# Scores from three stationary operands of at most three heads, with q gathered in two rounds and projected one iteration ahead

## The chip, the cores and the metric

The kernel runs on one core of one Trainium2 chip. The metric is the device time of one execution in microseconds. Engines are named as in the profile: PE is TensorE's matmul side and PEld its weight loads, DVE is VectorE, ACT is ScalarE, POOL is GpSimd, SP is the engine that issues DMAs.

## What is computed

Cross attention of 4 batches of 2048 query rows over 77 context rows, 16 heads of 32, everything in float32, followed by an output projection, a residual and a layer norm:

```python
qs = (q @ wq).reshape(Bq, Lq, H, HD).transpose(0, 2, 1, 3)
ks_ = (k @ wk).reshape(Bq, Lk, H, HD).transpose(0, 2, 1, 3)
vs = (v @ wv).reshape(Bq, Lk, H, HD).transpose(0, 2, 1, 3)
scores = jnp.einsum('bhqd,bhkd->bhqk', qs, ks_) / jnp.sqrt(jnp.float32(HD))
scores = jnp.where(mask[:, None, :, :], -jnp.inf, scores)
attn_w = jax.nn.softmax(scores, axis=-1)
attn = jnp.einsum('bhqk,bhkd->bhqd', attn_w, vs)
attn = attn.transpose(0, 2, 1, 3).reshape(Bq, Lq, H * HD)
out = attn @ wo + q
mu = jnp.mean(out, axis=-1, keepdims=True)
var = jnp.mean((out - mu) ** 2, axis=-1, keepdims=True)
return (out - mu) / jnp.sqrt(var + EPS) * gamma + beta
```

Here x has shape (4, 2048, 512), the context (4, 77, 512), and the four weights (512, 512).

## The kernel before

The 8192 query rows are 64 tiles of 128 rows (`T` = 64). Four tiles make a block of 512 rows; there are 16 blocks, and 16 tiles (`TB`) to a batch. All five engines run a program written out by hand, one iteration per tile t, and meet through semaphores only. Each engine executes its own list strictly in order.

Every float32 product is made of three products of shorter numbers: a matrix is split into a high part (x becomes `xh`, q becomes `qh`/`qn`, k becomes `khc`) and the low rest (`xl`, `ql`, `klc`), and high·high, high·low and low·high are added up in one PSUM bank.

In iteration t, PE does this:

- `scores(t, (0, 1))` and `scores(t, (2, 3))`: the scores of tile t, one group g of four heads at a time, into one of two banks.
- `project_q(i)`: 12 matmuls of 512 columns that make quarter m = i mod 4 of q for block i // 4. Four such calls make the q of one block. It waits for all four low slices of that block's x: `pe.wait_ge(g_xl, 4 * (i // 4 + 1))`.
- `project_o(t - 6)`: 12 matmuls of 512 columns, the output projection of an older tile.
- `weigh_v`: in iterations with t mod 4 = 1 (from 5), the attention-weighted values of four older tiles.
- `transpose_p(t - 1, half)`: five transposes each, of the normalised weights.

An iteration has two places for a projection: the first after `scores(t, (0, 1))`, the second after `scores(t, (2, 3))`. For t mod 4 = 0, 1, 2 the first holds `project_o(t - 6)` and the second `project_q(t + 4)`; for t mod 4 = 3 it is `project_q(t + 4)` first and `project_o(t - 6)` second.

ACT rounds x to `xh` (`keep_x(t + 8)`), copies q out of PSUM (`keep_q`), copies transposes and values, and computes the exponentials. DVE masks the scores and takes their maximum (`mask_max`, L789 and L795), sums rows and takes reciprocals (`row_sums`, L802 and L804), makes the low parts of q and of the values (`low_q` L777, `low_a` L811) and adds the residual. POOL runs, in iteration t, `deviation(t - 7)` (L990 to L996), `normalise(t - 1, 1)` (L977, L979), `gain_and_shift(t - 8)` (L1001, L1003), `low_x(t + 8)` (L962, the low slice of x) and `normalise(t, 0)`.

From block 2 on, one group of scores takes three matmuls: low q against high k, all four heads, 308 columns (L463), and twice 154 columns for two heads each (L469), where the stationary operand `qd` holds the high q of two heads twice over, and the moving operand `kd` holds their high k above their low k. `double_q(i)` builds `qd` with four DMAs per quarter of q; `place_kh` and `place_kd` build the k operands of a batch with DMAs. All of them are issued by SP, whose list also has the loads of x (`load_slice(t + 9)`, L260), the residual rows, the masks and the stores.

Of the kernel before, what the change touches and what calls it, by code (L numbers as in the profile page):

```python
# [11 lines left out]
GW = 4 * LK  # L12
PW = 2 * LK
NG = 4
HH = H // 2
# [23 lines left out]
LAG = 6  # L39

KD_AT = {4: 0, 12: 1, TB + 4: 2, 2 * TB + 4: 3}

KH_AT = {8: 1, TB + 8: 2, 2 * TB + 8: 3}
# [20 lines left out]
def cross_attention_layernorm(nc, x, xT, ctxT, mask, wq, wk, wv, wo, gamma, beta, out):  # L64
# [12 lines left out]
    with ctx:  # L77
# [13 lines left out]
        kh = sb("kh", [P, NG + 2, GW], f32r)  # L91
        kd = sb("kd", [P, 2, NG, 2, PW], f32r)
# [23 lines left out]

        ql0 = sb("ql0", [P, NG, D], f32r)
        ql1 = sb("ql1", [P, NG, D], f32r)


        with ExitStack() as start:
# [6 lines left out]
            early("place_qd", [P, 2 * NG * D - KT * D - KT * NB * LK])  # L128
# [7 lines left out]
            early("place_qn", [P, KT, D])  # L136
# [5 lines left out]
        qd = sb("qd", [P, 2, 2, NG, D], f32r)  # L142
        qn = sb("qn", [P, NG, D], f32r)
# [5 lines left out]
        ql = (ql0, ql1)  # L149
# [3 lines left out]
        qk = [ah, qd[:, 1, 0]] + [qn] * (NBLK - 2)  # L153

        kl = kd[:, 1].rearrange("p g u k -> p g (u k)")

        def kh_at(b, g):

            return g if g < 2 else g + 2 * (b % 2)
# [33 lines left out]
        d_kh = [sem(f"d_kh{i}") for i in range(2)]  # L193
        d_kl, d_kd = sem("d_kl"), [sem(f"d_kd{i}") for i in range(2)]
        d_qd = [sem(f"d_qd{g}") for g in range(NG)]
# [56 lines left out]
        def _(sp):  # L252
# [35 lines left out]
            def spread(dst, src, sig):  # L288

                for j in range(4):  # L290
                    rows = slice(32 * j, 32 * j + 32)
                    sp.dma_start(dst[rows, :, j * LK:(j + 1) * LK].bitcast(f32), src[rows].bitcast(f32)).then_inc(sig, 16)

            def place_kh(b, i):

                if i == 0:
                    sp.wait_ge(p_s, NG * (TB * b - 1) + 2)
                elif b >= 2:
                    sp.wait_ge(p_s, NG * TB * (b - 1))
                at = kh_at(b, 2 * i)  # L300
                spread(kh[:, at:at + 2], khc[:, 2 * i:2 * i + 2, b], d_kh[i])

            def place_kd(b):

                if b >= 1:
                    sp.wait_ge(p_s, NG * max(8, TB * (b - 1)))
                for v, src in enumerate((khc, klc)):
                    for j in range(4):
                        rows = slice(64 * v + 32 * (j % 2), 64 * v + 32 * (j % 2) + 32)
                        sp.dma_start(kd[rows, b % 2, :, j // 2, j % 2 * LK:(j % 2 + 1) * LK].bitcast(f32),  # L310
                                     src[32 * j:32 * j + 32, :, b].bitcast(f32)).then_inc(d_kd[b % 2], 16)

            def double_q(i):

                blk, m = i // 4, i % 4
                if blk >= 3:
                    sp.wait_ge(p_s, NG * 4 * (blk - 1))
# [17 lines left out]
            spread(kh[:, 0:NG], khc[:, :, 0], d_kh[0])  # L335
# [739 lines left out]
```

## Time and profile before

| | us |
|---|---|
| median of 3 runs | 617.94 (617.9 to 618.48) |
| profiled execution: span from the first to the last instruction | 616.2 |
| median less this span | 1.7 |
| PE busy in it | 599.4 (97%) |
| DVE, ACT, POOL busy | 520.4, 506.6, 491.3 |

The span covers the instructions; the time of an execution has some more around it. A row of a timeline gives the start in microseconds from the span's start, the duration, the engine, the line, the operation with out<-in, and how many equal instructions the row merges; in brackets stands the idle time before it and what ended that. PE's durations are latencies and overlap: the distance from one start to the next is what a matmul costs.

### The profile page before, as it was taken

How to read it: one execution, taken by the hardware profiler on the slowest of the kernel's cores; microseconds unless marked ns; L12 is line 12 of the kernel's file. 1: busy time of each engine (PE TensorE's matmuls, PEld its weight loads, DVE VectorE, ACT ScalarE, POOL GpSimd, SP SyncE). 2: the span in 40 equal slices, each digit the busy share in tenths (PEclk: the TensorE clock that was granted, in tenths of full speed). 3: DMA queues.
4: the chain of work that ended last, by engine and by line, in shares of the span. 5: the costliest groups of instructions: out<-in, count | busy, mean ns of one | idle time of the engine just before them, and what ended most of it. 6: DMA issues, size and time to landing. Idle time of an engine off the chain costs nothing.

```text
span 616.2 us, 12956 instructions
## 1 busy us (share of the span) xinstructions
PE 599.4 (97%) x3856; PEld 476.5 (77%) x3856; DVE 520.4 (84%) x1060; ACT 506.6 (82%) x1558; POOL 491.3 (80%) x639
## 2 busy tenths in 40 slices
PE   9998999999999999999999999999999999998995
PEld 7876687877878787787878788787878878786763
DVE  6677798898888889888888988898888889888888
ACT  6788888988888898888889888888988888886851
POOL 4587458897979889797979979797997979687784
PEclk9999999999999999999999999999999999999999
DMA  8621475463655546355654645555463555643103
GB/s 281 198 67 52 131 192 178 124 187 111 170 146 160 171 141 180 106 171 143 164 165 120 180 129 168 149 160 159 123 176 116 163 151 138 206 106 102 53 36 119
DMA packets 62165, 89.22 MB, mean 145 GB/s; under 512 B 20368, under 2 KB 20880, under 8 KB 62096
## 3 DMA queue, kind: packets, MB, share of 16 engines
q1 hardware_dynamic: 62096, 88.39, 50.1%
q8 instruction: 32, 0.52, 0.4%
q14 instruction: 37, 0.30, 0.1%
HBM read 39.53 MB, written 16.78 MB: 91 GB/s over the span
## 4 chain that ended last, share of the span: by engine, by line
PE 82%; DVE 6%; POOL 4%; ACT 4%; issue 2%; POOLq 0%; DVEq 0%; ACTq 0%
PE bank L433 27%; PE bank L529 24%; PE bank L479 7%; PE bank L469 6%; PE bank L463 5%; PE bank L502 4%; PE bank L483 2%; PE bank L507 2%; ACT pr L639 2%; PE bank L409 1%; DVE al L811 1%; PE bank L460 1%; ACT ah L607 1%; POOL pn L977 1%; DVE pr L789 1%
## 5 line engine op out<-in xcount | busy, mean ns | idle before, releaser
L639 ACT ACTIVATE pr<-pr,nm 128x77 f32<-128x77 f32 x1024 | 270.0, 349 | 39.5 <-DVE nm L795 35.9
L977 POOL TENSOR_TENSOR pn<-pr,rec 128x512 f32<-128x512 f32 x128 | 134.8, 1053 | 77.7 <-DVE rec L804 76.1
L789 DVE SCALAR_TENSOR_TENSOR pr<-msk,bank 128x308 f32<-128x308 uint8 x256 | 109.3, 468 | 33.6 <-PE bank L469 28.6
L802 DVE TENSOR_REDUCE sm<-pr 128x8 f32<-128x616 f32 x128 | 100.6, 786 | 9.7 <-ACT pr L639 9.3
L795 DVE TENSOR_REDUCE nm<-pr 128x8 f32<-128x616 f32 x128 | 101.7, 795 | 4.4
L529 PE MATMUL bank<-woh,ah 128*128 128x512 f32 x256 | 103.8, 405 | 1.4 <-DVE al L811 1.3
L433 PE MATMUL bank<-xh,wqh 128*128 128x512 f32 x256 | 103.2, 403 | 0.0
L607 ACT ACTIVATE ptr<-bank 128x512 f32<-128x512 f32 (+1 forms) x256 | 95.7, 428 | 8.8 <-PE bank L479 8.7
L529 PE MATMUL bank<-woh,al 128*128 128x512 f32 x256 | 101.3, 396 | 0.0
L529 PE MATMUL bank<-wol,ah 128*128 128x512 f32 x256 | 101.1, 395 | 0.0
L433 PE MATMUL bank<-xh,wql 128*128 128x512 f32 x256 | 100.3, 392 | 0.0
L433 PE MATMUL bank<-xl,wqh 128*128 128x512 f32 x256 | 100.0, 391 | 0.0
L463 PE MATMUL bank<-kh,ql 128*128 128x308 f32 x224 | 82.4, 368 | 2.2 <-DVE pr L789 2.2
L962 POOL TENSOR_TENSOR xl<-xraw,xh 128x512 fp32r<-128x512 f32 x58 | 75.5, 1303 | 10.1 <-ACT xh L607 10.0
L479 PE MATMUL bank<-ident,pn 128*128 128x128 f32 x512 | 77.0, 273 | 4.9 <-ACT ptr L607 3.5
L479 PEld LDWEIGHTS bank<-ident,pn 128*128 128x128 f32 x512 | 61.9, 140 | 21.6 <-issue 5.4
L469 PE MATMUL bank<-kd,qd 128*128 128x154 f32 x448 | 77.4, 254 | 0.0
L1003 POOL TENSOR_TENSOR y<-y,bet 128x512 f32<-128x512 f32 x56 | 72.2, 1290 | 4.4
L469 PEld LDWEIGHTS bank<-kd,qd 128*128 128x128 f32 x448 | 74.6, 190 | 0.0
L1001 POOL TENSOR_TENSOR y<-y,gam 128x512 f32<-128x512 f32 x56 | 72.1, 1288 | 0.0
L662 ACT ACTIVATE y<-z,rs 128x512 f32<-128x512 f32 x56 | 45.8, 817 | 30.7 <-POOL rs L996 29.6
L811 DVE TENSOR_TENSOR al<-bank,ah 128x512 fp32r<-128x512 f32 (+1 forms) x68 | 40.6, 642 | 26.8 <-ACT ah L607 26.8
(94 smaller groups left out, 1020.5 us busy)
## 6 DMA issues: line engine op xcount, KB each, us to landing
qd<-qn SPq DMA_DIRECT2D x224, 128.0 KB, 2.6
xraw<-xT SPq DMA_DIRECT2D x58, 256.0 KB, 3.4
xres<-x SPq DMA_DIRECT2D x58, 256.0 KB, 2.8
out<-y SPq DMA_DIRECT2D x56, 256.0 KB, 2.0
ptr<-xT SPq DMA_DIRECT2D x6, 256.0 KB, 9.0
zt<-x SPq DMA_DIRECT2D x6, 256.0 KB, 4.1
out<-zt SPq DMA_DIRECT2D x6, 256.0 KB, 2.0
wk_sb<-wk SPq DMA_DIRECT2D x4, 256.0 KB, 4.8
```

What stands on the lines that cost most here:

```text
L433: last = nc.tensor.matmul(misc_bank(("q", i))[:], w[:, k, m * P:(m + 1) * P], s[:, blk % 2, k, :], start=(k == 0 and n == 0), stop=(k == K ...
L463: nc.tensor.matmul(o[:, 0:GW], ql[blk % 2][:, g, cols], kh[:, kh_at(t // TB, g), :], start=True, stop=False)
L469: last = nc.tensor.matmul(o[:, u * PW:(u + 1) * PW], qd[:, blk % 2, u, g, cols], kd[:, t // TB % 2, g, u, :], start=False, stop=(u == 1))
L479: last = nc.tensor.transpose(PTB[0][:, s * P:(s + 1) * P], pn[:, half, s, :], ident[:])
L529: last = nc.tensor.matmul(o[:], w[:, k, r * P:(r + 1) * P], s[:, k, :], start=(n == 0), stop=(w is al and i == KT - 1))
L607: return nc.scalar.activation(dst, src, ACT.Copy)
L639: last = nc.scalar.activation(s, s, ACT.Exp, bias=nm[:, t % 2, h:h + 1], scale=1.0)
L789: nc.vector.scalar_tensor_tensor(out=pr[:, 4 * g:4 * g + 4, :], in0=msk[:, m % MR, t % 4, :].unsqueeze(1).broadcast_to([P, 4, LK]), scalar ...
L795: nc.vector.tensor_reduce(nm[:, t % 2, HH * half:HH * half + HH], pr[:, HH * half:HH * half + HH, :], AX.X, ALU.max, negate=True).then_inc ...
L802: nc.vector.tensor_reduce(sm[:, t % 2, hs], pr[:, hs, :], AX.X, ALU.add).then_inc(v_sum, 1)
L962: nc.gpsimd.tensor_tensor(xl[:, n // KT % 2, n % KT, :], x_of(n), xh[:, n // KT % 2, n % KT, :].bitcast(f32), ALU.subtract).then_inc(g_xl, 1)
L977: nc.gpsimd.tensor_tensor(pn[:, half, 0:4, :].rearrange("p s (e k) -> p (s e) k", e=2), pr[:, hs, 0:KM], rec[:, t % 2, hs].unsqueeze(2).br ...
```

## The change

- **Scores.** From block 2 on, the three stationary operands lie in `qs[:, buffer, part]`, 128 rows made of four 32-row pieces each. Part 0 holds high q of heads 0, 1, 2 and again of head 1; part 1 holds low q of heads 0, 1, 2 and high q of head 0; part 2 holds high q of head 3, its low q, its high q again, and high q of head 2. The moving operand `ks` has nine segments of 78 columns (`KW`, one more than 77). The three matmuls of a group then have 156, 234 and 234 columns.
- **Copies of q.** ACT and DVE write `qh` and `ql` straight into parts 0 and 1. `gather_q(i)` makes four copies of 32 rows into part 2; `fill_q(i)` waits for these to land and makes two more copies over the rows that were read. That is six DMAs of 64 KB per quarter in place of four of 128 KB.
- **Copies of k.** `place_k` makes twelve DMAs per batch, for batch 0 all twelve at the end of SP's iteration 4, for the others in two parts of six.
- **q projection.** From t = 3 on, the second place of an iteration holds `project_q(t + 5)` and the first `project_o(t - 6)`, also for t mod 4 = 3. Iteration 3 gets one projection more, and `project_o(54)` moves from after `scores(60, (0, 1))` into the second place of iteration 59. `keep_q(t + 4)` and `low_q(t + 4)` follow in iteration t. `low_x`, `keep_x` and `load_slice` stay where they are.
- The first two blocks keep their three matmuls over four heads, with 312 columns where there were 308.

```diff
+SA, SC, SH = 0, 3, 5
+K_PARTS = [(0, SC + 1, 3, 0), (1, SC + 1, 3, 0), (2, SC + 1, 3, 1), (3, SC, 2, 1),
+           (0, SA, 0, 0), (1, SA + 1, 1, 0), (2, SA + 2, 2, 0), (3, SA, 0, 0),
+           (0, SH, 0, 1), (1, SH + 1, 1, 0), (2, SH + 2, 2, 0), (3, SH + 1, 1, 1)]
+KN = len(K_PARTS)
+KS_AT = {4: (0, 0, KN), 10: (1, 0, KN // 2), 12: (1, KN // 2, KN)}
...
         for t in range(T - 4):
-            if t % 4 == 3:
+            if t <= 3:
                 misc += [("q", t + 4)]
             misc += [("o", t - LAG)] if t >= LAG else []
             misc += [("v", VALUES[t])] if t in VALUES else []
-            if t % 4 < 3:
-                misc += [("q", t + 4)]
+            if 3 <= t < T - 5:
+                misc += [("q", t + 5)]
...
+            def gather_q(i):
+
                 sp.wait_ge(a_qh, i + 1)
+                copy_q(i, 2, 0, 0, 3, d_qc)
+                copy_q(i, 2, 2, 0, 3, d_qc)
+                copy_q(i, 2, 3, 0, 2, d_qc)
+                sp.wait_ge(v_ql, i + 1)
+                copy_q(i, 2, 1, 1, 3, d_qc)
+
+            def fill_q(i):
+
+                sp.wait_ge(d_qc[i % 4], 64 * (i // 4 - 1))
+                copy_q(i, 1, 3, 0, 0, d_qa)
+                copy_q(i, 0, 3, 0, 1, d_qa)
...
-                if t in KD_AT:
-                    place_kd(KD_AT[t])
...
-                if 5 <= t <= T - 4 and t % 4 > 0:
-                    double_q(t + 3)
...
+                if 4 <= t < T - 4:
+                    gather_q(t + 4)
...
+                if 4 <= t < T - 4:
+                    fill_q(t + 4)
...
+                if t in KS_AT:
+                    place_k(*KS_AT[t])
...
-                    nc.tensor.matmul(o[:, 0:GW], ql[blk % 2][:, g, cols], kh[:, kh_at(t // TB, g), :], start=True, stop=False)
...
-                    for u in range(2):
-                        last = nc.tensor.matmul(o[:, u * PW:(u + 1) * PW], qd[:, blk % 2, u, g, cols],
-                                                kd[:, t // TB % 2, g, u, :], start=False, stop=(u == 1))
...
+                    for n, (part, head, seg, heads) in enumerate(((2, 2, SC, 2), (1, 0, SA, 3), (0, 0, SH, 3))):
...
+                        last = nc.tensor.matmul(o[:, KW * head:KW * (head + heads)], qs[:, blk % 2, part, g, cols],
+                                                ks[:, t // TB % 2, g, seg:seg + heads, :].rearrange("p h k -> p (h k)"),
+                                                start=(n == 0), stop=(n == 2), skip_group_check=True)
...
-                if t % 4 == 3:
+                if t == 3:
                     project_q(t + 4)
                 elif t >= LAG:
                     project_o(t - LAG)
...
-                if t % 4 == 3:
-                    if t >= LAG:
-                        project_o(t - LAG)
+                if t < 3:
+                    project_q(t + 4)
+                elif t == T - 5:
+                    project_o(T - 10)
                 elif t >= LAG or t not in VALUES:
-                    project_q(t + 4)
+                    project_q(t + 5)
...
-            project_o(T - 10)
```

PE in iteration 11 (t mod 4 = 3) before: the end of `project_q(15)` in the first place, the transposes (L479, L483), the scores (L463, L469), and the start of `project_o(5)` (L529) in the second place:

```order
L433 MATMUL bank<-xl,wqh 128x512
L433 MATMUL bank<-xh,wql 128x512
L479 MATMUL bank<-ident,pn 128x128 [waits a_pt,g_norm]
L479 MATMUL bank<-ident,pn 128x128 x3
L483 MATMUL bank<-ident,pn 128x128
L463 MATMUL bank<-kh,ql 128x308 [waits v_st,v_ql]
L469 MATMUL bank<-kd,qd 128x154 x2
L463 MATMUL bank<-kh,ql 128x308 [waits v_st,v_ql]
L469 MATMUL bank<-kd,qd 128x154 x2
L529 MATMUL bank<-woh,ah 128x512 [waits v_al,v_ql]
L529 MATMUL bank<-wol,ah 128x512
```

The same stretch of iteration 11 in the changed kernel, where L523 is `project_o(5)` and L424 is `project_q(16)`, the first quarter of block 4:

```order
L523 MATMUL bank<-wol,ah 128x512
L523 MATMUL bank<-woh,al 128x512
L473 MATMUL bank<-ident,pn 128x128 [waits a_pt,g_norm]
L473 MATMUL bank<-ident,pn 128x128 x3
L477 MATMUL bank<-ident,pn 128x128
L462 MATMUL bank<-ks,qs 128x156 [waits v_st]
L462 MATMUL bank<-ks,qs 128x234 x2
L462 MATMUL bank<-ks,qs 128x156 [waits v_st]
L462 MATMUL bank<-ks,qs 128x234 x2
L424 MATMUL bank<-xh,wqh 128x512 [waits g_xl,v_ql]
L424 MATMUL bank<-xl,wqh 128x512
```

The second place now holds the first quarter of the next block, which waits on `g_xl`, POOL's count of low slices; before, this quarter stood in the second place of iteration 12.

SP in iterations 4 and 5 before, from the load of slice 13 of x to the load of slice 15 (the `vm` and `vr` rows place the values of batch 3):

```order
L260 DMA xraw<-xT 128x512 [waits g_xl]
L310 DMA kd<-khc 32x4x77 x4
L310 DMA kd<-klc 32x4x77 x4
L271 DMA msk<-mask 128x308 [waits v_st]
L260 DMA xraw<-xT 128x512 [waits g_xl]
L321 DMA qd<-qn 64x512 [waits a_qh]
L321 DMA qd<-qn 64x512 x3
L265 DMA xres<-x 128x512 [waits p_v]
L265 DMA xres<-x 128x512
L280 DMA vm<-vs 64x4x64 [waits a_v]
L285 DMA vr<-vs 13x2x32 x4
```

SP in iteration 4 of the changed kernel, from the last gather copy of q(8) to the load of slice 14 (the first L255 row of iteration 5):

```order
L301 DMA qs<-qs 32x512 [waits v_ql]
L266 DMA msk<-mask 128x308 [waits v_st]
L301 DMA qs<-qs 32x512 [waits d_qc0]
L301 DMA qs<-qs 32x512
L296 DMA ks<-khc 32x4x77 [waits g_z]
L296 DMA ks<-khc 32x4x77
L296 DMA ks<-klc 32x4x77 x2
L296 DMA ks<-khc 32x4x77 x4
L296 DMA ks<-klc 32x4x77
L296 DMA ks<-khc 32x4x77 x2
L296 DMA ks<-klc 32x4x77
L255 DMA xraw<-xT 128x512 [waits g_xl]
```

Ahead of the load of slice 14 stand now six copies of q and twelve of k in place of eight of k; the copies of q(9) and the rest of iteration 5 come behind it in both.

## Rows read from the trace of the kernel before

**Rows 1.** The page: busy time by engine, and the chain that ended last
```profile
PE 599.4 (97%) x3856; PEld 476.5 (77%) x3856; DVE 520.4 (84%) x1060; ACT 506.6 (82%) x1558; POOL 491.3 (80%) x639
...
PE 82%; DVE 6%; POOL 4%; ACT 4%; issue 2%; POOLq 0%; DVEq 0%; ACTq 0%
```
**Rows 2.** Timeline: weight loads of one group of scores
```profile
305.04 0.19 PEld L463 LDWEIGHTS bank<-kh,ql 128*128 128x128 f32 x1
...
305.15 0.34 PEld L469 LDWEIGHTS bank<-kd,qd 128*128 128x128 f32 x2
...
305.41 0.19 PEld L529 LDWEIGHTS bank<-woh,ah 128*128 128x128 f32 x1
...
305.52 0.19 PEld L529 LDWEIGHTS bank<-wol,ah 128*128 128x128 f32 x1
```
**Rows 3.** Timeline of PE: values, and the second place of iteration 31
```profile
280.73 1.95 PE L502 MATMUL bank<-ptr,vm 64*32 64x512 f32 x32
...
301.39 0.44 PE L529 MATMUL bank<-woh,ah 128*128 128x512 f32 x1
...
304.24 0.60 PE L479 MATMUL bank<-ident,pn 128*128 128x128 f32 x4
```
**Rows 4.** Timeline of POOL, iterations 29 to 31
```profile
288.26 1.05 POOL L977 TENSOR_TENSOR pn<-pr,rec 128x512 f32<-128x512 f32 x1 [3.24 <-DVE rec L804]
...
303.08 1.29 POOL L962 TENSOR_TENSOR xl<-xraw,xh 128x512 fp32r<-128x512 f32 x1
304.61 1.05 POOL L977 TENSOR_TENSOR pn<-pr,rec 128x512 f32<-128x512 f32 x1 [0.23 <-DVE rec L804]
```
**Rows 5.** Timeline of ACT and DVE in iteration 29
```profile
283.73 2.07 ACT L607 ACTIVATE ah<-bank 128x512 fp32r<-128x512 f32 x4 [0.60 <-PE bank L507]
...
284.36 1.29 DVE L811 TENSOR_TENSOR al<-bank,ah 128x512 fp32r<-128x512 f32 x2 [1.83 <-ACT ah L607]
...
287.97 0.20 DVE L804 RECIPROCAL rec<-sm 128x8 f32<-128x8 f32 x1
```
**Rows 6.** Timeline of PE and POOL: second place and low_x, iterations 11 and 55
```profile
122.31 0.43 PE L529 MATMUL bank<-woh,ah 128*128 128x512 f32 x1
...
123.96 1.30 POOL L962 TENSOR_TENSOR xl<-xraw,xh 128x512 fp32r<-128x512 f32 x1
...
516.28 0.44 PE L529 MATMUL bank<-woh,ah 128*128 128x512 f32 x1
...
518.00 1.30 POOL L962 TENSOR_TENSOR xl<-xraw,xh 128x512 fp32r<-128x512 f32 x1
```
**Rows 7.** Timeline of SP, iterations 4 and 5
```profile
60.99 3.00 SPq L310 DMA_DIRECT2D kd<-khc  x4
...
67.74 0.43 SPq L260 DMA_DIRECT2D xraw<-xT  x1
68.21 2.46 SPq L321 DMA_DIRECT2D qd<-qn  x4
...
77.16 0.44 SPq L260 DMA_DIRECT2D xraw<-xT  x1
```
**Rows 8.** The page's DMA issues: KB each, median us to landing
```profile
qd<-qn SPq DMA_DIRECT2D x224, 128.0 KB, 2.6
xraw<-xT SPq DMA_DIRECT2D x58, 256.0 KB, 3.4
```
**Rows 9.** Timeline of ACT, POOL and PE: slice 15 and iteration 7
```profile
83.21 0.63 ACT L607 ACTIVATE xh<-xraw 128x512 fp32r<-128x512 f32 x1
...
85.12 1.28 POOL L962 TENSOR_TENSOR xl<-xraw,xh 128x512 fp32r<-128x512 f32 x1
...
86.54 0.39 PE L529 MATMUL bank<-woh,ah 128*128 128x512 f32 x1
```
**Rows 10.** Timeline of PE in iteration 61: a wait near the end
```profile
566.39 0.38 PE L463 MATMUL bank<-kh,ql 128*128 128x308 f32 x1 [1.30 <-DVE pr L789]
```
**Rows 11.** Windows of PE at the end: us, busy, granted clock, DMA share, GB/s
```profile
610.00:614.00 4.00, 0.33 (x2) 1.00 0.35 131
614.00:616.20 2.20, 0.00 (x0) 0.60 0.32 119
```

More of the change, by code:

```diff
@@ L11 @@
 TB = LQ // P
-GW = 4 * LK
-PW = 2 * LK
 NG = 4
+KW = LK + 1
 HH = H // 2
@@ L39 @@
 LAG = 6
-KD_AT = {4: 0, 12: 1, TB + 4: 2, 2 * TB + 4: 3}
-KH_AT = {8: 1, TB + 8: 2, 2 * TB + 8: 3}
+SA, SC, SH = 0, 3, 5
[4 more added lines that the diff above has]
+KS_AT = {4: (0, 0, KN), 10: (1, 0, KN // 2), 12: (1, KN // 2, KN)}
+for _b in (2, 3):
+    KS_AT |= {TB * (_b - 1) + 4: (_b, 0, KN // 2), TB * (_b - 1) + 8: (_b, KN // 2, KN)}
 V_AT = {1: (1,), 3: (2, range(0, 2)), 4: (2, range(2, 4))}
@@ L148, in cross_attention_layernorm @@
         y = sb("y", [P, YS, D])
-        ql = (ql0, ql1)
         wkh = woh
[L153 to L159, printed above, removed]
+        qh = [ah] + [qs[:, blk % 2, 0] for blk in range(1, NBLK)]
+        ql = [qs[:, 0, 2]] + [qs[:, blk % 2, 1] for blk in range(1, NBLK)]
         def x_of(n):
@@ L192, in cross_attention_layernorm @@
         d_y = [sem(f"d_y{i}") for i in range(YS)]
-        d_kh = [sem(f"d_kh{i}") for i in range(2)]
-        d_kl, d_kd = sem("d_kl"), [sem(f"d_kd{i}") for i in range(2)]
-        d_qd = [sem(f"d_qd{g}") for g in range(NG)]
+        d_kh, d_kl = sem("d_kh"), sem("d_kl")
+        d_ks = [sem(f"d_ks{i}") for i in range(2)]
+        d_qc = [sem(f"d_qc{g}") for g in range(NG)]
+        d_qa = [sem(f"d_qa{g}") for g in range(NG)]
         d_end, d_xe = sem("d_end"), sem("d_xe")
@@ L286, in place_v, with spread @@
                                          vs[at + KM - lo:at + LK - lo, i, s, e]).then_inc(d_vb[b], 16)
-            def spread(dst, src, sig):
+            def spread(seg, src, sig):
                 for j in range(4):
                     rows = slice(32 * j, 32 * j + 32)
[L292 to L301, printed above, removed]
@@ L303, in place_kd @@
-            def place_kd(b):
-                if b >= 1:
-                    sp.wait_ge(p_s, NG * max(8, TB * (b - 1)))
[L307 to L317, printed above, removed]
-                sp.wait_ge(a_qh, i + 1)
-                for u in range(2):
-                    for v in range(2):
-                        sp.dma_start(qd[64 * v:64 * v + 64, blk % 2, u, m].bitcast(f32), qn[64 * u:64 * u + 64, m].bitcast(f32)
-                                     ).then_inc(d_qd[m], 16)
+                    sp.dma_start(ks[rows, 1, :, seg + j, 0:LK].bitcast(f32), src[rows, :, 0].bitcast(f32)).then_inc(sig, 16)
@@ new lines, in place_k, with copy_q @@
+            def place_k(b, first, end):
+                if b == 0:
+                    sp.wait_ge(g_z, 2)
+                else:
+                    sp.wait_ge(p_s, NG * max(8, TB * (b - 1)))
+                for row, seg, head, low in K_PARTS[first:end]:
+                    sp.dma_start(ks[32 * row:32 * row + 32, b % 2, :, seg, 0:LK].bitcast(f32),
+                                 (khc, klc)[low][32 * head:32 * head + 32, :, b].bitcast(f32)).then_inc(d_ks[b % 2], 16)
+            def copy_q(i, to, row, of, head, sig):
+                q, m = qs[:, i // 4 % 2], i % 4
+                sp.dma_start(q[32 * row:32 * row + 32, to, m].bitcast(f32),
+                             q[32 * head:32 * head + 32, of, m].bitcast(f32)).then_inc(sig[m], 16)
@@ L400, in _ @@
             for i in range(8):
-                nc.tensor.matmul(bank[7][:], ql0[:, 0, 0:P], ql0[:, 0, :], start=True, stop=True)
+                nc.tensor.matmul(bank[7][:], ql[0][:, 0, 0:P], ql[0][:, 0, :], start=True, stop=True)
             for k in range(KT):
@@ L709, in _ @@
                     keep_v(V_KEPT[t])
-                if t % 4 > 0:
+                if t >= 4:
+                    keep_q(t + 4)
+                elif t > 0:
                     keep_q(t + 3)
@@ L880, in _ @@
                 if t in VALUES:
-                    low_q(t + 3)
+                    low_q(t + 4)
                 if t >= 1:
                     mask_max(t, 0)
-                if t % 4 > 0 and t not in VALUES:
+                if 1 <= t <= 3:
                     low_q(t + 3)
+                elif t >= 4 and t not in VALUES:
+                    low_q(t + 4)
                 if t in VALUES:
@@ L890, in _ @@
                 mask_max(t, 1)
[L891 removed]
+                if t == 3:
                     low_q(t + 4)
```

67 lines of the change are left out of this document (28 added, 39 removed).

## The prediction

> **What bounds the kernel now.** I read the page first: PE is busy for 97% of the span, and the chain that ended last lies on PE for 82% of it [rows 1]. Then I asked the timeline of PE for its gaps in the middle of the run and found hardly any: from iteration 9 to 60 matmul follows matmul. From the second place of iteration 11 to that of 55 it is 516.28 - 122.31 = 394.0 us [rows 6], 35.8 us for four iterations. So a microsecond taken from PE there is a microsecond won, and a microsecond that PE has to wait there is lost. The other engines are no idle bystanders: POOL works 80% of the time, and the question for every move is whether what PE will now ask for earlier is there earlier.
>
> **Part 1, the scores.** The timeline of PE's weight loads shows what a group of scores costs [rows 2]. A group begins with the load for L463 at 305.04; the next load starts 0.11 us later, the two loads of L469 fill the time to 305.41, and the first load of the projection follows. The group takes 0.37 us. Behind a short matmul the next load comes 0.11 us after the one before (305.04 to 305.15, and 305.41 to 305.52), although 154 columns need less: there the weight load is the limit. Behind the 308 columns it is the columns, about 0.15 us. So the group is 0.15 + 0.11 + 0.11. In the new one, 156 columns are surely under the load's 0.11. 234 columns are three quarters of 308, 0.11 us, so just at the same limit. The new group costs 3 x 0.11 = 0.33 us, perhaps 0.34. I take a gain of 0.035 us; bounds are 0.05 and, if a 234-column matmul pays both load and a part of its columns, 0. Blocks 2 to 15 have 14 x 16 = 224 groups: 7.8 us if all of them counted.
> The Trainium skill (TensorE: Matmul & The Clock Gate, "LDWEIGHTS" and "Back-to-back issue gap") gives 107 ns for a load of 128 columns and N/2.4 + 2.5 ns for the columns, 100 ns for 234. By it a group would cost 0.32 us and gain 0.05, 11 us over all groups. The load agrees with the trace's 0.11, no row has 234 columns, and the sum below goes by the rows.
>
> **Part 2, q one iteration ahead.** This is where I expect the time to go. The order of PE shows that for t mod 4 = 3 the second place now holds the first quarter of the next block's q. It needs all four low slices of x of that block. For t = 31 this is `project_q(36)`, and the last slice is `low_x(39)`, which POOL makes in the same iteration 31; its place was not moved. Before, that quarter came an iteration later.
> PE reaches the second place of iteration 31 at 301.39 [rows 3]. POOL starts `low_x(39)` at 303.08 and ends it 1.29 us later, at 304.37 [rows 4]. PE would wait for 2.98 us. It is the same at the first and last of these iterations: 122.31 against 123.96 + 1.30, and 516.28 against 518.00 + 1.30, 2.95 and 3.02 us [rows 6]. Twelve iterations are alike (11, 15, ... 55).
> Can POOL come earlier? Not by working ahead. From 288.26 to 304.37 it has no gap worth the name; that is 16.1 us of its own work [rows 4]. The start of that stretch is set by a reciprocal on DVE (288.17), behind the low part of the values, which waited 1.83 us for ACT's copy, which in turn waited 0.60 us for PE's L507 of `weigh_v` [rows 5]. The chain therefore begins at PE's own `weigh_v` of iteration 29 (280.73 [rows 3]) and takes a fixed time, however long PE stands later. It starts again in every fourth iteration, because POOL waits 3.24 us for it there and carries no lead over. A faster PE between `weigh_v` and the second place only waits longer: of the 16 groups of four iterations, ten lie in that stretch and win nothing, six win.
> Behind the waiting projection are PE's transposes of t - 1, the next tile's scores, and with them DVE, ACT and the next `weigh_v`. So every wait goes into the end. Price: 12 x 2.98 = 35.8 us. When the slice lands, the first weight load is exposed as well, 0.11 us [rows 2], 1.3 us in all. The gain of part 1 counts for 224 - 120 = 104 groups: 3.6 us.
>
> **Part 3, SP at the start.** SP issues in order, and up to iteration 7 it is late as it is. Eight copies of k cost 0.75 us each (3.00 for four [rows 7]) ahead of the load of slice 14 at 67.74. Now there are twelve of them, 9.0 us, and ahead of these four gather copies at 0.6 us (2.46 for four), a wait until they have landed (2.6 us from the issue of the last [rows 8]) of which the mask covers 0.6, and two fills, 1.2 us. From 60.99: gathers to 63.5, landed at about 65.5, fills to 66.7, k to 75.7. Slice 14 is issued 8 us late. Iteration 5 took 9.4 us to slice 15 (67.74 to 77.16) and has two fills more: 75.7 + 10.6 = 86.3. Add 3.4 us to landing [rows 8], 0.63 on ACT and 1.28 on POOL [rows 9]: slice 15 is ready at 91.6. PE needs it for `project_q(12)` in the second place of iteration 7, which it reached at 86.54 [rows 9]. That is 5.1 us once. The extra projection of iteration 3, 2.85 us by the length of one (301.39 to 304.24 [rows 3]), is PE time before this point and vanishes in the same wait. The price of a 32-row copy is unknown: if it is half of a 64-row one the shift is about 3 us; if the delay is passed on to slices 16 and 17 it is 9.
>
> **Costed at nothing.** The copies of q(4b + 3): its low part is ready in the middle of iteration 4b - 1 and its scores are due in the middle of 4b, 8 us and a stall later; two rounds at 2.6 us and six issues at 0.6 us take 8 us at most. If this cover were gone, it would cost a few tenths per block. Six k copies (4.5 us of SP) in later batches stand in front of loads that are needed two iterations later. DVE reads scores with a step of 78 where it was 77, in a read of the same four pieces. The projection taken out of iteration 60 wins at most its 2.85 us; near the end PE waits for DVE anyway (1.30 us in iteration 61 [rows 10]), so I take 1 us.
>
> **Sum.** On the profiled span: 616.2 + 35.8 + 1.3 + 5.1 - 3.6 - 1.0 = 653.8 us. The median lies 1.7 us above the span, which gives 655.5.
>
> **Rivals.**
> - *Stall and a lower clock.* In each stall PE is idle for about 3.3 us (2.98 plus ten groups' gain), longer than anywhere in the run now. The granted clock stands at 1.00 through the window to 614.0, whose last matmul work ends after 0.33 us, and averages 0.60 after that [rows 11]: nearly 4 us of idleness left it at 2.4 GHz, more brought 1.2 GHz. That speaks against a fall at 3.3 us, but closely. One projection at half clock costs 2.85 us more; in all twelve stalls 34 us, about 690; in a few of them 660 to 670. The Trainium skill (TensorE: Matmul & The Clock Gate, "Why this matters for your kernels") warns that gaps between bursts of matmuls bring the lower clock back; by that rule this case would hold at every stall.
> - *Half a stall.* Something in POOL's 16.1 us shortens once PE stands still, or slice 15 is not late. With half the stall, 655.5 - 18 = 638.
> - *Faster.* PE does not wait in the second place at all; this needs the slice 3.0 us earlier in every block, that is POOL's chain from `weigh_v` to `low_x` in 20.6 us (283.73 to 304.37) shrunk to 17.6. Then all 7.8 us count and the start costs 0 to 5: 610 to 616. Break-even with the rest as forecast is a stall below 0.2 us. The rows say nothing for it: POOL alone needs 16.1.
> - *Scores cost no less.* If 234 columns behind a load cost 0.13 us, the 3.6 us vanish: 659, inside the forecast.
>
> **Chances.** Forecast as described (643 to 665) 0.70; with a lower clock beyond that (665 to 690) 0.12; half a stall (625 to 643) 0.12; faster or unchanged 0.06. The range for 8 in 10 goes from 637 to 670. A difference of 0.2% (1.2 us) is about what a measurement of this kernel can tell; slower by more than that 0.93, within it 0.02, faster 0.05.
>
> **What the changed kernel's profile would show.** In the chain of waits, PE waiting for POOL's xl, twelve to thirteen times, 3 us each and about 40 us in total; in the timeline, the first L424 of a block starting right after the end of POOL's xl. The distance from one `weigh_v` to the next in the middle of the run is 35.8 + 2.98 + 0.11 - 6 x 0.035 = 38.7 us. Weight loads of a scores group 0.11 us apart, a group 0.33 us. At the start, POOL's slice 15 ends near 92 and the load of slice 15 is issued near 86 instead of 77. Granted clock 1.00 throughout. I am wrong if POOL's xl in iteration t mod 4 = 3 ends before PE arrives, if PE waits for qs or ks copies instead, or if the stalls come with a lower clock.

## The result, and the profile after

The changed kernel takes 677.38 us (median of 4 runs, 676.03 to 678.32) where the kernel before took 618.1 us beside it: a ratio of 1.0955 (95% interval 1.0939 to 1.0971), 59.3 us slower. Medians in this document leave out two executions that stand apart, 1512.09 us of the order alone at full clock and 662.04 us of the kernel before at a granted clock of 0.851. The forecast was 655.5 us, at most 670. Its sign and the wait that it named were right; the lower clock that comes with that wait, a rival with a chance of 0.12, is missing from its sum.

The page of the changed kernel, with the lines that answer to [rows 1]. A group's line gives busy time, the mean of one in ns, and after the second bar the idle time just before it with what ended most of it.

```profile
PE 616.6 (91%) x3856; PEld 484.2 (72%) x3856; DVE 521.6 (77%) x1060; ACT 510.6 (76%) x1558; POOL 493.3 (73%) x640
...
PEclk9999979989998998999999899999989999998998
...
PE 57%; DVE 13%; POOL 12%; issue 6%; SPq 5%; ACT 4%; DMA 2%; POOLq 0%; DVEq 0%
...
L424 PE MATMUL bank<-xh,wqh 128*128 128x512 f32 x256 | 108.9, 425 | 43.5 <-POOL xl L958 43.5
```

Three things have changed. PE is busy for 91% of the span instead of 97%. The chain now lies on PE for only 57%; DVE and POOL, which feed the wait, have come into it. And the row of the granted clock, nines throughout before, has sevens and eights in it: in those slices TensorE ran at 1.2 GHz for a while. The mean granted clock is 0.968.

The chain of waits of PE (us in total, times, longest) has one entry that towers over the rest:

```profile
PE bank L424 <- POOL xl L958: 43.5, 14, 6.5
PE bank L473 <- ACT ptr L601: 2.0, 3, 0.8
PE bank L462 <- DVE pr L782: 2.0, 4, 1.0
```

L424 is the first matmul of `project_q`, L958 is `low_x`. The longest of the 14 waits, 6.5 us, is at the start; twelve of about 3.0 us follow, one in every fourth iteration. PE in iteration 31, in the timeline (start, duration, in brackets the idle time before it and its releaser), against [rows 3]:

```profile
331.07 0.92 PE L462 MATMUL bank<-ks,qs 128*128 128x156 f32 x6
334.98 0.47 PE L424 MATMUL bank<-xh,wqh 128*128 128x512 f32 x1 [2.99 <-POOL xl L958]
335.29 0.39 PE L424 MATMUL bank<-xl,wqh 128*128 128x512 f32 x1
335.52 0.43 PE L424 MATMUL bank<-xh,wql 128*128 128x512 f32 x1
335.76 0.63 PE L424 MATMUL bank<-xh,wqh 128*128 128x512 f32 x1
336.18 0.63 PE L424 MATMUL bank<-xl,wqh 128*128 128x512 f32 x1
...
339.40 0.60 PE L473 MATMUL bank<-ident,pn 128*128 128x128 f32 x4
```

POOL ahead of it, against [rows 4]:

```profile
330.99 1.28 POOL L997 TENSOR_TENSOR y<-y,gam 128x512 f32<-128x512 f32 x1
332.35 1.26 POOL L999 TENSOR_TENSOR y<-y,bet 128x512 f32<-128x512 f32 x1
333.57 1.27 POOL L958 TENSOR_TENSOR xl<-xraw,xh 128x512 fp32r<-128x512 f32 x1
```

POOL ends `low_x(39)` at 333.57 + 1.27 = 334.84, and PE starts 0.14 us later after 2.99 us of idleness. This is the wait of the forecast, though not measured in the same way: the forecast counts from the start that the next matmul would have had, the profile's idle time from the end of the last one. What the forecast left out stands behind it: from 335.76 on the matmuls are 0.42 to 0.43 us apart instead of 0.23, and the projection takes 339.40 - 334.98 = 4.42 us. The windows of PE in iteration 27, which had a wait of 3.00 us just before 296.17, and in iteration 31 (columns: stretch, PE busy, granted clock, DMA share, GB/s):

```profile
296.00:297.00 1.00, 0.83 (x4) 1.00 0.78 260
297.00:298.00 1.00, 1.00 (x6) 1.00 0.95 289
...
335.00:336.00 1.00, 1.00 (x4) 0.87 0.79 277
336.00:337.00 1.00, 1.00 (x3) 0.50 0.96 299
337.00:338.00 1.00, 1.00 (x4) 0.50 0.57 207
338.00:339.00 1.00, 1.00 (x4) 0.50 0.11 37
339.00:340.00 1.00, 1.00 (x8) 0.92 0.00 0
```

The same wait is followed by full clock in iteration 27 and by 3.4 us of 1.2 GHz in iteration 31. The clock fell in this way after 8 of the 12 waits, each time for 3.41 us. The four iterations from one `weigh_v` to the next take 40.3 to 40.4 us with such a stretch and 38.75 to 38.9 without, so a stretch costs 1.55 us.

SP at the start, against [rows 7]:

```profile
61.96 3.11 SPq L301 DMA_DIRECT2D qs<-qs  x4
...
76.11 0.59 SPq L255 DMA_DIRECT2D xraw<-xT  x1
...
87.32 0.43 SPq L255 DMA_DIRECT2D xraw<-xT  x1
```

and what it leads to on ACT:

```profile
93.23 0.63 ACT L601 ACTIVATE xh<-xraw 128x512 fp32r<-128x512 f32 x1 [7.17 <-DMA xraw<-xT]
```

Slice 14 is issued at 76.11 and slice 15 at 87.32 (forecast 75.7 and 86.3). ACT can start on slice 15 at 93.23, so the load took 5.9 us from issue to use, not 3.4.

**Where 60.1 us of span went (676.3 - 616.2).** I use `weigh_v` of iterations 9 and 57 as marks. Its matmuls in the kernel before:

```profile
L502 PE MATMUL bank<-ptr,vm x32: 588/589/614, 101.6 to 103.0; 64*32 64x512 f32 x32
...
L502 PE MATMUL bank<-ptr,vm x32: 589/589/614, 531.4 to 532.8; 64*32 64x512 f32 x32
```

and in the changed kernel (`to` stands between the starts of the first and the last):

```profile
L496 PE MATMUL bank<-ptr,vm x32: 589/589/613, 112.6 to 113.9; 64*32 64x512 f32 x32
...
L496 PE MATMUL bank<-ptr,vm x32: 589/589/613, 590.5 to 591.9; 64*32 64x512 f32 x32
```

The start has lost 112.6 - 101.6 = 11.0 us. Twelve cycles of four iterations now take 477.9 us instead of 429.8: 48.1 us more. A low clock of 8 x 1.55 = 12.4 us is part of this, and 35.7 us are left, 2.97 per cycle. The tail, from the second mark to the end, has lost 1.0 us.

### The profile page after: what moved, and what is told of

Its sections match the earlier page's. It is cut to its first block, busy times and chain, and to the rows that moved or that the text cites. A ratio compares the mean times of both kernels' runs of the same rounds, so it can differ in the third digit from the quotient of the medians.

```text
span 676.3 us, 12773 instructions
## 1 busy us (share of the span) xinstructions
PE 616.6 (91%) x3856; PEld 484.2 (72%) x3856; DVE 521.6 (77%) x1060; ACT 510.6 (76%) x1558; POOL 493.3 (73%) x640
## 4 chain that ended last, share of the span: by engine, by line
PE 57%; DVE 13%; POOL 12%; issue 6%; SPq 5%; ACT 4%; DMA 2%; POOLq 0%; DVEq 0%
PE bank L424 20%; PE bank L523 18%; PE bank L462 6%; PE bank L473 5%; PE bank L496 4%; POOL pn L973 3%; POOL xl L958 3%; DVE pr L782 2%; POOL y L997 2%; DVE nm L788 2%; PE bank L501 2%; SPq L280 2%; PE bank L477 2%; ACT pr L630 2%; POOL pn L975 2%
## 5 line engine op out<-in xcount | busy, mean ns | idle before, releaser
L424 PE MATMUL bank<-xh,wqh 128*128 128x512 f32 x256 | 108.9, 425 | 43.5 <-POOL xl L958 43.5
L424 PE MATMUL bank<-xl,wqh 128*128 128x512 f32 x256 | 106.5, 416 | 0.0
L424 PE MATMUL bank<-xh,wql 128*128 128x512 f32 x256 | 106.0, 414 | 0.0
L462 PE MATMUL bank<-ks,qs 128*128 128x234 f32 (+1 forms) x672 | 103.2, 290 | 2.0 <-DVE pr L782 2.0
L523 PE MATMUL bank<-woh,ah 128*128 128x512 f32 x256 | 103.2, 403 | 1.5 <-DVE al L804 1.4
L523 PE MATMUL bank<-woh,al 128*128 128x512 f32 x256 | 102.2, 399 | 0.0
L523 PE MATMUL bank<-wol,ah 128*128 128x512 f32 x256 | 102.2, 399 | 0.0
L462 PEld LDWEIGHTS bank<-ks,qs 128*128 128x128 f32 x672 | 84.4, 192 | 14.3 <-issue 11.4
L424 PEld LDWEIGHTS bank<-xh,wqh 128*128 128x128 f32 x256 | 50.4, 197 | 55.7 <-issue 45.9
L958 POOL TENSOR_TENSOR xl<-xraw,xh 128x512 fp32r<-128x512 f32 x58 | 75.1, 1295 | 17.5 <-ACT xh L601 17.4
L473 PE MATMUL bank<-ident,pn 128*128 128x128 f32 x512 | 78.5, 276 | 3.6 <-ACT ptr L601 2.0
L473 PEld LDWEIGHTS bank<-ident,pn 128*128 128x128 f32 x512 | 63.7, 142 | 21.3 <-issue 5.6
L601 ACT ACTIVATE qs<-bank 128x512 fp32r<-128x512 f32 x60 | 35.1, 585 | 42.6 <-PE bank L424 42.6
L424 PEld LDWEIGHTS bank<-xh,wql 128*128 128x128 f32 x256 | 51.5, 201 | 12.8
```

The costliest lines, as they stand in the source:

```text
L424: last = nc.tensor.matmul(misc_bank(("q", i))[:], w[:, k, m * P:(m + 1) * P], s[:, blk % 2, k, :], start=(k == 0 and n == 0), stop=(k == K ...
L462: last = nc.tensor.matmul(o[:, KW * head:KW * (head + heads)], qs[:, blk % 2, part, g, cols], ks[:, t // TB % 2, g, seg:seg + heads, :].re ...
L473: last = nc.tensor.transpose(PTB[0][:, s * P:(s + 1) * P], pn[:, half, s, :], ident[:])
L523: last = nc.tensor.matmul(o[:], w[:, k, r * P:(r + 1) * P], s[:, k, :], start=(n == 0), stop=(w is al and i == KT - 1))
L601: return nc.scalar.activation(dst, src, ACT.Copy)
L958: nc.gpsimd.tensor_tensor(xl[:, n // KT % 2, n % KT, :], x_of(n), xh[:, n // KT % 2, n % KT, :].bitcast(f32), ALU.subtract).then_inc(g_xl, 1)
```

## Experiments: is it the order, and what does the clock cost?

My theory was that nearly everything comes from `project_q` asking for `xl` too early; the rival was the new scores with their six copies per quarter. Four kernels ran beside the kernel before (618.0 us).

**Scores alone.** The new operands and copies, with q projected in the old order:

```diff
-            if t <= 3:
+            if t % 4 == 3:
                 misc += [("q", t + 4)]
...
-                if 4 <= t < T - 4:
-                    gather_q(t + 4)
+                if 5 <= t <= T - 4 and t % 4 > 0:
+                    gather_q(t + 3)
+                    if t % 4 == 3 and t < T - 4:
+                        gather_q(t + 4)
```

> The change with the q projection, keep_q and low_q back in the order of before; the three new stationary operands, gather and fill stay. Theory (the new order makes PE wait about 3.0 us for POOL's low slice in every fourth iteration, and the idleness brings the lower clock): no wait on xl in iterations t mod 4 = 3, granted clock 1.00 in the middle, a scores group 0.33 us, and so 618 - 7.8 plus at most 0.5 us per block for a late fill of q(4b+3): 611 to 619 us. Rival (the new operands or their copies cost the time): 640 us or more, with PE waiting for qs or ks.

Measured: 631.85 us, ratio 1.0229 (1.0196 to 1.0261). The expected time was missed by some 12 us. In the middle PE waits for no `xl`, and from iteration 17 on a cycle takes 35.6 to 35.9 us, at most 36.4. The loss is at the start: `weigh_v` of iteration 9 stands at 109.6, 8.0 us late, and the cycle after it takes 39.8 us, 4.0 more than before. Two stretches of 1.2 GHz of 3.41 us lie there, at 93.6 and 141.4. The largest of PE's waits up to the mark are these:

```profile
93.55 1.08 PE L477 MATMUL bank<-ident,pn 128*128 128x128 f32 x4 [3.43 <-ACT ptr L605]
...
101.00 0.56 PE L466 MATMUL bank<-ks,qs 128*128 128x234 f32 x3 [1.02 <-DMA qs<-qs]
```

ACT works in order. It stands at the late slice, the copies of P behind it are late too, and PE waits for those. So the SP queue costs its microseconds without the new q order as well.

**Order alone.** The scores of the kernel before, and only q one iteration ahead:

```diff
-                if t % 4 == 3:
+                if t == 3:
                     project_q(t + 4)
...
-                if t % 4 == 3:
-                    if t >= LAG:
-                        project_o(t - LAG)
+                if t < 3:
+                    project_q(t + 4)
+                elif t == T - 5:
+                    project_o(T - 10)
                 elif t >= LAG or t not in VALUES:
-                    project_q(t + 4)
+                    project_q(t + 5)
```

> The kernel before with the q projection one iteration ahead and nothing else; its scores with 308, 154, 154 columns stay. Theory: the same twelve waits of about 3.0 us and low clock after most of them: 618 + 36 + 1 + about 17, and a few us at the start, 670 to 680 us. Rival (the operands and copies cost the time): within 5 us of 618.

Measured: 670.24 us, ratio 1.0848 (1.0815 to 1.088). Of the 59.3 us, 52.2 come with this part alone:

```profile
PE bank L431 <- POOL xl L964: 36.2, 13, 2.9
```

Thirteen waits of 2.9 us at most, 0.1 less than with the new scores. The granted clock is 0.975, and it fell after 8 of the twelve waits in the middle here too. The two parts alone (13.9 + 52.2) come to 7 us more than both at once. The late start explains little of that: by the mark of iteration 9 it is 8.0 us with the scores alone and 3.7 with the order alone, against 11.0. In the twelve cycles the scores alone lose 3.7 us where I expected a gain, and the order alone 49.0, against 48.1 for both.

**The idle time filled.** Twelve matmuls on constant weights, written to a bank that the projection then overwrites, keep PE busy while it waits:

```diff
                     misc_free(pe, ("q", i))
+                    if i % 4 == 0 and i >= 12:
+                        for n in range(12):
+                            nc.tensor.matmul(misc_bank(("q", i))[:], wqh[:, n % KT, 0:P], wql[:, n % KT, :], start=True, stop=True)
                     pe.wait_ge(g_xl, 4 * (i // 4 + 1))
```

> The changed kernel with 12 matmuls of 512 columns on constant weights added ahead of the wait on g_xl in the first quarter of each block from block 3 on; their result is overwritten, so the output stays the same. They take 2.8 us and fit into the wait of 3.0. Theory (the wait itself brings the lower clock): no low clock in the middle, the distance between blocks stays at 38.7 us everywhere instead of 38.7 or 40.4, total 656 to 662 us. Rival (the lower clock has another cause, such as the shorter matmuls of the scores): still about 677, low clock as before. If the added matmuls themselves cost, more than 677.

Measured: 662.63 us, ratio 1.0719 (1.0694 to 1.0745), 14.8 us less than the changed kernel, with more work on PE. The added matmuls move no slice forward; they take away only the idleness. The row of the clock is at full speed but for the start:

```profile
PEclk9999989999999999999999999999999999999999
...
L499 PE MATMUL bank<-ptr,vm x32: 589/589/613, 110.2 to 111.5; 64*32 64x512 f32 x32
...
L499 PE MATMUL bank<-ptr,vm x32: 589/589/613, 575.6 to 576.9; 64*32 64x512 f32 x32
```

By these marks the twelve cycles take 465.4 us instead of 477.9, 12.5 less, which agrees with the 12.4 counted from the eight stretches. The tail takes 1.5 less; no stretch of 1.2 GHz falls into PE's work there. The start takes 2.4 less, of which 0.7 is clock (the stretch in which PE works lasts 3.41 us here and 4.9 there, at half speed) and 1.8 is a slice that landed earlier in this execution. The low clock that filling takes away is thus 12.5 + 1.5 + 0.7 = 14.7 us of the 59.3, and the medians differ by 14.8.

**The slice first.** POOL makes `low_x(t + 8)` ahead of `gain_and_shift` instead of behind it:

```diff
                     normalise(t - 1, 1)
+                if t + 8 < 4 * NBLK:
+                    low_x(t + 8)
                 if t == LAG + 2:
                     pool.wait_ge(d_gb, 32)
                 if t >= LAG + 2:
                     gain_and_shift(t - LAG - 2)
-                if t + 8 < 4 * NBLK:
-                    low_x(t + 8)
```

> The changed kernel with one move on POOL: low_x(t + 8) goes ahead of gain_and_shift(t - 8), 2.6 us earlier. Theory: the wait in iterations t mod 4 = 3 shrinks from 3.0 to about 0.3 to 0.5 us, the low clock in the middle is gone: 677.4 - 12 x 2.6 - 8 x 1.7, 630 to 636 us; the loss at the start stays. Rival (PE's wait is set by something else than POOL's place of the slice): 670 or more.

Measured: 633.6 us, ratio 1.0246 (1.0228 to 1.0265). PE in iteration 31:

```profile
313.77 0.61 PE L462 MATMUL bank<-ks,qs 128*128 128x234 f32 x4
314.81 0.47 PE L424 MATMUL bank<-xh,wqh 128*128 128x512 f32 x1 [0.43 <-POOL xl L958]
```

The two operations of `gain_and_shift` held the slice back for 2.6 us; moving it past them shortens the wait from 2.99 to 0.43, and in the middle the clock never falls. 12 x 2.56 + 12.4 = 43.1 us were to be won by this count. The twelve cycles take 434.7 us, 43.2 less, and the medians differ by 43.8.

## Experiments: the start, and a version that works

Beside these the kernel before took 618.02 us.

**K placed early.** The twelve copies of k for batch 0 move from SP's iteration 4 to ahead of its loop, where SP had nothing to issue from 22.5 to 31.0 us:

```diff
-KS_AT = {4: (0, 0, KN), 10: (1, 0, KN // 2), 12: (1, KN // 2, KN)}
+KS_AT = {10: (1, 0, KN // 2), 12: (1, KN // 2, KN)}
...
+            place_k(0, 0, KN)
             for t in range(T + LAG):
```

> The changed kernel with the twelve k copies of batch 0 issued before SP's iteration 0, into a gap of 8.5 us that SP's list has there (22.5 to 31.0), instead of at the end of its iteration 4. Theory (SP's lateness makes slices 14 to 16 late and PE wait 6.5 us in iteration 7, with a low clock after it): slice 15 comes 8 us earlier, PE's wait in iteration 7 falls below 1 us and its low clock goes; the twelve later waits stay: 677.4 - 6 - 3.4, 665 to 670 us. Rival (the loss at the start comes from the added projection or the copies of q): 674 to 677.

Measured: 667.03 us, ratio 1.0794 (1.0775 to 1.0813), 10.4 us less than the changed kernel. Of the start's 11.0 us, 9.1 are gone (`weigh_v` of iteration 9 stands at 103.5); another 1.6 us come from the tail, where the stretch of 1.2 GHz of the last projections is missing. The waits in the middle stay:

```profile
PE bank L425 <- POOL xl L959: 36.5, 13, 3.1
```

Twelve of them take 2.95 to 3.06 us, one 0.9, and the low stretch at the start is not there any more.

**Scores alone, k early.** The same edit in the kernel with the scores alone:

> The new scores in the old order of projections, with the k copies of batch 0 issued before SP's iteration 0. Theory: what scores_only lost (631.9 against 618) was lost at the start; without it the gain of the scores, 224 groups x 0.035 = 7.8 us, shows, less a few waits for late fills: 611 to 617 us. Rival (the new operands cost in the middle as well): above 620.

Measured: 625.4 us, ratio 1.0112 (1.0073 to 1.0151): missed by 8 us. With the old order two quarters of q are gathered and filled in one iteration, twelve DMAs one behind the other on SP, and PE waits for them:

```profile
PE bank L467 <- DMA qs<-qs: 4.1, 7, 1.1
PE bank L478 <- ACT ptr L606: 3.4, 4, 1.0
```

These waits, and a stretch of 1.2 GHz at 133.9, lie mostly between the marks: twelve cycles take 434.4 us, and 426.7 in the last kernel of this part (616.34 us), which has the same scores and the new order. So the new scores seem to want the new order: q one iteration ahead gives the two rounds of copies their time, and PE's waits for `qs` fall from 4.1 us in total to 0.5. The two kernels differ in POOL's order as well.

**Slice first for all, k early.** Both repairs together:

> slice_first (low_x ahead of gain_and_shift) and the early k copies together. Theory: both losses are separate and add up: 633.6 - 9 to 11, 622 to 626 us, with about 0.5 us of waiting left in each block.

Measured: 623.63 us, ratio 1.009 (1.0067 to 1.0114). What is left of the waits is 0.4 us each (12 of them are 4.7 us):

```profile
PE bank L425 <- POOL xl L959: 4.7, 12, 0.5
```

This is the chain of waits between 100 and 600 us.

**Slice first where it is needed.** `low_x` goes ahead of `normalise(t - 1, 1)` and `gain_and_shift`, but only for t mod 4 = 3, with k early:

```diff
                     deviation(t - LAG - 1)
+                if t % 4 == 3 and t + 8 < 4 * NBLK:
+                    low_x(t + 8)
                 if t >= 1:
                     normalise(t - 1, 1)
...
-                if t + 8 < 4 * NBLK:
+                if t % 4 != 3 and t + 8 < 4 * NBLK:
                     low_x(t + 8)
```

> Early k copies, and low_x(t + 8) ahead of normalise(t - 1, 1) in iterations t mod 4 = 3 alone, 1.4 us earlier than in slice_first; in the other iterations low_x stays behind gain_and_shift. Theory: the slice ends at about 1 us before PE asks for it, no wait on xl in the middle, no low clock, and the full gain of the scores: 612 to 618 us. Rival (POOL's later normalise makes PE's transposes wait instead): 620 or more.

Measured: 616.34 us (median of 9), ratio 0.9974 (0.9961 to 0.9986): faster than the kernel before by 1.7 us, a quarter of a per cent. POOL's slice, and PE in the second place of iteration 31:

```profile
299.90 1.30 POOL L959 TENSOR_TENSOR xl<-xraw,xh 128x512 fp32r<-128x512 f32 x1
```

```profile
301.41 0.92 PE L463 MATMUL bank<-ks,qs 128*128 128x156 f32 x6
302.16 0.40 PE L425 MATMUL bank<-xh,wqh 128*128 128x512 f32 x1
```

The slice ends at 301.20, PE asks for it at 302.16 and doesn't wait. From k early to this kernel only POOL's order differs, and it is 667.03 - 616.34 = 50.7 us. A cycle takes 35.55 us instead of 35.82. The twelve cycles win 3.1 us against the kernel before and the tail 0.7, while the start still loses 2.2 (its mark stands at 103.8). What the scores gain can be read here, undisturbed, against [rows 2]:

```profile
305.39 0.75 PEld L463 LDWEIGHTS bank<-ks,qs 128*128 128x128 f32 x6
306.06 0.19 PEld L524 LDWEIGHTS bank<-woh,ah 128*128 128x128 f32 x1
```

Six loads in 306.06 - 305.39 = 0.67 us for two groups, 0.73 before: 0.033 per group, 7.3 us over 224. A cycle of 16 groups should win 0.53 and wins 0.27. The other half, 0.26 per cycle, went elsewhere.

## Experiments: where half of the scores' gain went

In the traces, the 512-column matmuls of `project_q` start 229.1 ns apart (median) before and 233 ns in all kernels with the new scores; those of `project_o` 233.2 before and 233.9 after. 720 such matmuls by 4 ns are 2.9 us, 0.19 of the 0.26 per cycle. The new layout moves every tile behind `ks`, so I suspected the address of `xh` and `xl`: a multiple of 64 bytes before, 32 bytes beyond one after. Two kernels have an unused tile of 32 bytes per partition; beside them the kernel before took 618.23 us:

```diff
         kd = sb("kd", [P, 2, NG, 2, PW], f32r)
+        sb("pad", [P, 8])
         vm = sb("vm", [P, NB, 4, 2, HD])
```

> The kernel before with an unused tile of 32 bytes per partition behind kd, which moves all later tiles, xh and xl among them, from a multiple of 64 bytes to 32 beyond one, as they lie in the changed kernel. Theory (the place of xh and xl in memory makes each matmul of project_q start 233 ns after the last instead of 229, as in all kernels with the new layout): 233 ns per matmul of project_q, and 720 x 4 ns = 2.9 us more, about 620.9 us. Rival (the 4 ns come from the copies of q, or from the scores): 229 ns and 618.0.

Measured: 621.15 us, ratio 1.0047 (1.0034 to 1.0061), and the spacing of `project_q` is 233.2 ns instead of 229.1. No instruction differs, only addresses. One projection near iteration 31, its first and sixth matmul, 1.17 us for five distances:

```profile
300.71 0.40 PE L434 MATMUL bank<-xh,wqh 128*128 128x512 f32 x1
...
301.88 0.40 PE L434 MATMUL bank<-xh,wql 128*128 128x512 f32 x1
```

The same tile behind `ks` in the best version:

> slice2_k_early with the same 32 bytes behind ks, which puts xh and xl back on a multiple of 64 bytes. Theory: 229 ns per matmul of project_q and 2.9 us less than 616.3, 613 to 614 us; this would be the fastest version. Rival: still 233 ns and 616.

Measured: 616.29 us, ratio 0.9962 (0.995 to 0.9975), the same as without the tile (616.34). The rule of 64 bytes is refuted: `project_q` stays at 232.9 ns, and instead `project_o` falls from 233.9 to 230.1. That should be worth 2.7 us and is not found: a cycle takes 35.51 us instead of 35.56, and the profiled execution has a stretch of 1.2 GHz at 563.5 in the tail. That placement moves a 512-column matmul by 4 ns is shown, by which rule stays open, and so does whether placement is what slows `project_q` in the new layout; no kernel here brought it back to 229 ns.

## Experiments: how short an idle time brings the low clock?

The number of added matmuls sets how long PE is really idle. Both ran beside the kernel before at 617.46 us; the edit is that of the filled idle time with 2 or 5 in place of 12.

**Two matmuls.**

> fill_wait with 2 added matmuls instead of 12: PE is idle for about 2.5 us in each of the twelve waits instead of 3.0, and asks for the slice at the same time. Theory (only an idleness of about 3 us brings the lower clock): the low clock is gone or rare, and the time is that of fill_wait, 661 to 666 us. Rival (any idleness in this place does, or the low clock depends on the busy share over a longer stretch): most of the eight low stretches stay, 672 to 677 us.

Measured: 674.21 us, ratio 1.0918 (1.09 to 1.0935). My theory of these runs, that the low clock needs nearly the full 3 us, fell. PE in iteration 31:

```profile
330.71 0.63 PE L434 MATMUL bank<-wql,wqh 128*128 128x512 f32 x2
333.72 0.50 PE L424 MATMUL bank<-xh,wqh 128*128 128x512 f32 x1 [2.38 <-POOL xl L961]
...
334.76 0.40 PE L424 MATMUL bank<-xl,wqh 128*128 128x512 f32 x1
335.00 0.55 PE L424 MATMUL bank<-xh,wql 128*128 128x512 f32 x1
335.35 0.63 PE L424 MATMUL bank<-xh,wqh 128*128 128x512 f32 x1
335.78 0.63 PE L424 MATMUL bank<-xl,wqh 128*128 128x512 f32 x1
```

After 2.38 us of idleness and 1.4 us of full speed the distances go to 0.43 us all the same. It happens in 7 of the 12 cycles.

**Five matmuls.**

> fill_wait with 5 added matmuls: about 1.8 us of idleness in each wait. Theory: no low clock in the middle, 661 to 664 us. If fill_2 and this one both keep the low clock, a short idleness is enough.

Measured: 663.52 us, ratio 1.0746 (1.0719 to 1.0772), within a microsecond of the kernel with twelve. The waits between 100 and 600 us:

```profile
PE bank L424 <- POOL xl L961: 20.8, 12, 1.9
```

Twelve of 1.7 us on average and 1.9 us at most, and no low clock in the middle. For these twelve places the border lies between 1.9 and 2.4 us of idleness. But it is no border that an idle time could be held against elsewhere. In the tail of this same kernel the clock falls 0.2 us after an idle time of 1.82 us, in the middle of these matmuls:

```profile
610.02 1.48 PE L465 MATMUL bank<-ks,qs 128*128 128x156 f32 x6 [1.82 <-DVE pr L785]
```

With the order alone it falls at 89.4, after an idle time of 1.79 us that ended at 88.6, and with the scores alone and k early at 133.9, after two idle times of 1.15 and 0.71 us with 0.6 us of work between them.

## Why the prediction was wrong in size, point by point

- **The wait for `xl`: right.** Forecast 2.98 us twelve times, measured 2.99 in iteration 31 and 3.00 in iteration 27. That the numbers agree to 0.02 is partly luck: with the ten faster groups and the first weight load the forecast puts PE's delay at about 3.4 us, and the profile's idle time leaves out what two matmuls overlap. The fair comparison is the cycle at full clock, forecast 38.7 us and measured 38.8 (35.82 + 2.97). The argument that POOL's 16.1 us cannot shrink because they hang on `weigh_v` held. Slice first for t mod 4 = 3 shows the cause: 50.7 us from POOL's order alone.
- **"That speaks against a fall at 3.3 us, but closely": the step that failed.** I read in [rows 11] that nearly 4 us of idleness had left the clock at 2.4 GHz, and gave the lower clock a chance of 0.12. The row was one case at the end of the run. The clock answers to a single idle time of 3 us in some cycles and not in others (8 of 12), and to 2.4 us in 7 of 12. One instance that went well is no bound. The term stands at nothing in the sum. It should have stood there with 12.4 us in the middle, 2.4 at the start and 1.6 in the tail, 16.4 us; filling the idle time gave 14.8 of it back. My rival had the sizes "in a few of them 660 to 670, in all twelve about 690". It priced one at 2.85 us, a whole projection at half speed, where the stretch lasts 3.41 us and costs 1.55.
  The Trainium skill (TensorE: Matmul & The Clock Gate, "Why this matters for your kernels") warns of idle gaps above about 3 us between bursts of matmuls. The traces agree at 3.0 us, though not "at every stall" as I had spelled it out; where gaps of 2.4 us bring the low clock too, and at other places of these kernels gaps under 2 us, the measurement decides.
- **The start: right in kind, half in size.** Forecast 5.1 us, measured 11.0. Issue was only 1.0 us later than forecast, but the load took 5.9 us instead of 3.4, so `xl` ended at about 95.2, not 91.6: 3.6 us more. Then came 6.83 us of 1.2 GHz from 93.4 on; PE worked in it from 95.35 to 100.2, which costs 2.4. 5.1 + 3.6 + 2.4 = 11.1. The upper bound of 9 us that I gave did not include a clock. K placed early takes 9.1 of the 11.0 us away and confirms the cause.
- **The gain of the scores: right per group, half of it lost again.** Forecast 0.035, measured 0.033. Costed at nothing, and wrong: the matmuls of `project_q` start 4 ns further apart in the new layout, which takes 2.9 us of the 7.3; that the moved tiles do it is likely, not shown. In the changed kernel only 104 groups count, so this is within about a microsecond of the sum.
- **"The copies of q(4b + 3)": right** for this order. No PE wait for `qs` of any size stands in its middle. In the old order the same copies cost several microseconds.
- **The tail: wrong by 2 us.** Forecast a gain of 1.0, measured a loss of 1.0. It holds two stretches of 1.2 GHz, at 619.1 and 663.4. Without any ahead of PE's last matmul, in the kernel with the filled idle time, the tail takes 84.2 us, a gain of 0.6 on the 84.8 before. K placed early has a stretch at the first place alone and takes 84.1. So the one at 663.4, in the last projections, costs 1.6 us, and the other nothing.

Sum of the corrections on the forecast span of 653.8: 12.4 for the clock in the middle, 1.1 for the rest of the middle (35.7 against a forecast of 12 x 2.88 = 34.6), 11.0 - 5.1 = 5.9 at the start and 2.0 in the tail give 675.2, and 676.3 was measured. The 1.1 left are the part of the scores' gain that the sum had outside the twelve cycles (3.6 - 12 x 0.21); the losses at the start and in the tail are counted with it.

## What to carry to other kernels

Moving a projection one iteration ahead on PE is a change to POOL as well: whoever asks earlier must be served earlier. Here the change became a small gain once one POOL operation was moved in one iteration of four and twelve DMA issues went to a place where SP's queue was empty. Price an idle time on PE at its length plus the stretch of low clock that may follow, with a chance, and don't take one idle time without a fall, nor a length that passed in one place, as proof that others will do without. To find what a low clock costs, fill the wait with harmless matmuls and see how far the time falls.

## What the runs showed of the hardware that I had not expected

- After idle times of equal length, 3.0 us, the granted clock fell to 1.2 GHz in 8 of 12 cases, after 2.4 us in 7 of 12, after 1.7 to 1.9 us in none of 12. Elsewhere in the same kernels 1.8 us, and 1.15 and 0.71 us close together, were followed by a fall. Each fall in the middle lasts 3.41 us. It begins 0.8 us after PE has resumed work in iteration 31 of the changed kernel, and 1.4 us after in that with two added matmuls. What decides which wait is followed by one was not worked out here.
- An unused tile of 32 bytes per partition makes the kernel before 0.47% slower, by 4 ns on each matmul of `project_q`; in the best version it speeds up `project_o` by the same amount. The rule behind it stays open.
